# Feed-forward of a decoder layer: gate and up with waits of their own, one maximum over a row of 2048, the integers ahead of the fourth weighing

## The reference

```
def activation_quant(x):
    scale = 127.0 / clip(max(abs(x), axis=-1), EPS, None)
    return clip(round(x * scale), -128.0, 127.0) / scale
gate = bit_linear(x, w_gate)              # 512 -> 2048, x quantised, weights -1, 0, 1 times a scale
up = bit_linear(x, w_up)                  # 512 -> 2048
activated = up * square(relu(gate))
activated = activated * rsqrt(mean(square(activated)) + LN_EPS) * subln_weight
return bit_linear(activated, w_down)      # 2048 -> 512, activated quantised by its greatest magnitude
```

## Time and profile before

| | us |
|---|---|
| median of 3 runs | 669.22 (667.73 to 669.85) |
| the profiled execution, its own time | 666.3 |
| its span | 664.5 |

### The profile page before, as it was taken

One profiled execution on the slowest core, in us unless ns is written; L12 is line 12 of the kernel. 1 busy time (PEld: TensorE's weight loads), 2 busy tenths in 40 slices (PEclk: granted clock), 3 DMA queues, 4 the chain that ended last, 5 costly groups with the idle time before them and its releaser, 6 DMA issues.

```text
span 664.5 us, 10361 instructions
## 1 busy us (share of the span) xinstructions
PE 604.7 (91%) x2741; PEld 336.7 (51%) x2758; DVE 470.2 (71%) x919; ACT 462.7 (70%) x799; POOL 276.8 (42%) x263
## 2 busy tenths in 40 slices
PE   5899999999999998989999999994689999999976
PEld 3535454545364543357777777772244444444332
DVE  3456767575757474536787787789799998989860
ACT  2364666666666665238888889874689888888970
POOL 1000000101010000236777777752587777777761
PEclk9959999999999998889999999996899999999997
DMA  8563144545353627125566566542035354443434
GB/s 300 163 195 87 40 103 151 112 140 125 128 130 122 148 107 161 45 63 166 162 192 170 162 188 185 164 128 79 24 65 120 95 118 98 101 96 87 95 75 100
DMA packets 83752, 82.89 MB, mean 125 GB/s; under 512 B 46160, under 2 KB 57936, under 8 KB 83600
## 3 DMA queue, kind: packets, MB, share of 16 engines
q1 hardware_dynamic: 83728, 82.61, 46.2%
HBM read 47.51 MB, written 4.28 MB: 78 GB/s over the span
## 4 chain that ended last, share of the span: by engine, by line
PE 30%; DVE 8%; POOL 6%; issue 6%; DMA 2%; ACT 1%; DVEq 1%; POOLq 0%; ACTq 0%; SPq 0%
PE ps L713 21%; PE ps L1083 5%; PE ps L1098 4%; POOL big L1340 3%; DMA act8t<-ys 2%; DVE toep L1225 2%; POOL ys L1348 2%; DVE st L1177 1%; DVE qo L766 1%; DVE ot L1263 1%; DVE x_all L1172 1%; POOL r L1336 1%; DVE mb L1229 1%; ACT kv L1122 0%; ACT kv L1120 0%
## 5 line engine op out<-in xcount | busy, mean ns | idle before, releaser
L713 PE MATMUL ps<-kv,toep 128*128 128x288 f32 x640 | 157.3, 409 | 1.2 <-PEq L1411 1.1
L713 PEld LDWEIGHTS ps<-kv,toep 128*128 128x128 f32 x640 | 122.1, 191 | 36.3 <-issue 2.6
L1098 PE MATMUL ps<-wt,xqt 128*128 128x512 bf16 x496 | 119.5, 386 | 14.2 <-DVE toep L1225 6.8
L1340 POOL TENSOR_TENSOR big<-toep,wst 128x512 f32<-128x512 f32 x64 | 83.0, 1299 | 50.3 <-DVE toep L1225 50.3
L401 ACT ACTIVATE big<-ps,kscale 128x512 f32<-128x512 f32 x128 | 84.9, 695 | 13.7 <-PE ps L251 12.0
L251 PE MATMUL ps<-qx,kx 128*128 128x512 f32 x128 | 78.1, 638 | 11.2 <-ACT big L401 10.6
L1098 PEld LDWEIGHTS ps<-wt,xqt 128*128 128x128 bf16 x512 | 49.4, 99 | 75.9 <-DVE toep L1225 13.4
L766 DVE TENSOR_REDUCE qo<-big 128x2048 f32 (+1 forms) x32 | 72.2, 2257 | 0.0
L1083 PE MATMUL ps<-wt,act8t 128*128 128x512 bf16 x255 | 60.7, 392 | 9.0 <-DMA act8t<-ys 8.0
L701 POOL TENSOR_TENSOR kv<-ctx 128x768 f32<-128x768 f32 (+1 forms) x32 | 52.7, 1646 | 37.3 <-PE ps L713 28.4
L755 DVE TENSOR_TENSOR big<-ps,qd 128x1024 f32<-128x1024 f32 x32 | 39.2, 1224 | 37.2 <-ACT ys L845 34.8
(11 more groups left out here) (120 smaller groups left out, 968.2 us busy)
## 6 DMA issues: line engine op xcount, KB each, us to landing
qx<-kv SPq DMA_DIRECT2D x128, 128.0 KB, 2.4
wst<-in_wall SPq DMA_DIRECT2D x12, 1024.0 KB, 6.7
wst<-in_wall SPq DMA_DIRECT2D x48, 256.0 KB, 3.7
toep<-krows SPq DMA_DIRECT2D x32, 256.0 KB, 3.8
ctx<-in_ctxt SPq DMA_DIRECT2D x32, 192.0 KB, 2.6
out_y<-ot SPq DMA_DIRECT2D x16, 256.0 KB, 2.2
conv_part<-qo SPq DMA_DIRECT2D x14, 256.0 KB, 2.8
x_all<-in_x SPq DMA_DIRECT2D x2, 1536.0 KB, 14.6
```

The costliest lines, as they stand in the source:

```text
L713: mm = pe.matmul(m.ps[:, LB * r + lb, :].rearrange("p (b s) -> p b s", s=WIDE)[:, :, 0:PAIRS], m.toep[r][:, d * P:(d + 1) * P], m.kv[r][:, ...
L1098: mm = pe.matmul(bank[:, n % 2, :], xqt[r][:, k, :], wt[:, k, n * C:(n + 1) * C], start=(k == 0), stop=(k == CK - 1))
L1340: nc.gpsimd.tensor_tensor(act_w[r][:, n * C:(n + 1) * C], a[n % 2][:], gb[:, n * C:(n + 1) * C], ALU.mult).then_inc(s_w.sem, 1)
```

## The change

Gate's matmuls wait until relu has read the bank, up's until the product has. The guard of r2 that the old wait gave becomes a wait of its own ahead of the squaring on ACT. The four maxima of 512 columns and the small one over their results become one maximum over the row's 2048 columns, which stands between scale and scale_b. DVE's product of chunk 1 comes ahead of the statistics. POOL's integers of row t-1 come ahead of the fourth weighing of row t.

```
             for n in range(IC):
-                if n >= 2:
-                    wait(pe, s_a, t, n - 1)
-                elif after:
-                    wait(pe, s_a, t - 1, n + 3)
-                for bank, wt, s in ((GB, gate_w, s_g), (UB, up_w, s_u)):
+                for bank, wt, s, free in ((GB, gate_w, s_g, s_rl), (UB, up_w, s_u, s_a)):
+                    if n >= 2:
+                        wait(pe, free, t, n - 1)
+                    elif after:
+                        wait(pe, free, t - 1, n + 3)
                     for k in range(CK):
...
-        def relu(t, n):
+        def relu(t, n, after=True):
             wait(act, s_g, t, n + 1)
             act.activation(rl[n % 2][:], GB[:, n % 2, :], ACT.Relu).then_inc(s_rl.sem, 1)
             wait(act, s_rl, t, n + 1)
+            if n >= 2:
+                wait(act, s_a, t, n - 1)
+            elif after:
+                wait(act, s_a, t - 1, n + 3)
             act.activation(r2[n % 2][:], rl[n % 2][:], ACT.Square).then_inc(s_r2.sem, 1)
...
-        def greatest(t, n, r):
-            wait(dve, s_w, t, n + 1)
-            nc.vector.tensor_reduce(mb4[:, n:n + 1], act_w[r][:, n * C:(n + 1) * C], AX.X, ALU.max,
-                                    apply_absolute_value=True).then_inc(s_mb4.sem, 1)
+        def greatest(t, r):
+            wait(dve, s_w, t, IC)
+            nc.vector.tensor_reduce(mb[:], act_w[r], AX.X, ALU.max, apply_absolute_value=True).then_inc(s_mb.sem, 1)
...
-            wait(dve, s_mb4, t, IC)
-            nc.vector.tensor_reduce(mb[:], mb4[:], AX.X, ALU.max).then_inc(s_mb.sem, 1)
...
             if rows:
                 rows_x2(t + 2)
-            if after:
-                greatest(t - 1, 3, 1 - r)
+            chunk(t, 1, after)
             if rows:
                 rows_stats(t + 2)
-            chunk(t, 1, after)
             if after:
                 scale(t - 1, 1 - r)
             if rows:
                 rows_mean(t + 2)
                 rows_var(t + 2)
             if after:
-                wait(dve, s_mb, t - 1, 1)
-            greatest(t, 0, r)
-            if after:
+                greatest(t - 1, 1 - r)
                 scale_b(t - 1, 1 - r)
             chunk(t, 2)
-            greatest(t, 1, r)
             if rows:
                 rows_norm(t + 2)
             chunk(t, 3)
             if rows:
                 rows_greatest(t + 2)
                 rows_scale(t + 2)
-            greatest(t, 2, r)
...
-        greatest(NT - 1, 3, 1)
+        greatest(NT - 1, 1)
         scale(NT - 1, 1)
...
             weigh(t, 2, r)
-            weigh(t, 3, r)
             if after:
                 integers(t - 1, 1 - r, after=last and final_first)
+            weigh(t, 3, r)
```

More of the change, by code:

```diff
@@ L944, in ffn @@
     act8t = two("act8t", [P, FK, P], BF16)
-    mb4 = sb("mb4", [P, IC])
     cc, sm, var, r4, cr, mb, bm, rb, qs = (sb(n, [P, 1]) for n in (
@@ L960, in ffn @@
     s_x32, s_xq, s_xqt, s_xqe = (sig(n) for n in ("x32", "xq", "xqt", "xqe"))
-    s_g, s_u, s_rl, s_r2, s_a, s_as, s_w, s_mb4 = (sig(n, IC) for n in ("g", "u", "rl", "r2", "a", "as", "w", "mb4"))
+    s_g, s_u, s_rl, s_r2, s_a, s_as, s_w = (sig(n, IC) for n in ("g", "u", "rl", "r2", "a", "as", "w"))
     s_sm, s_cc, s_var, s_r4, s_mb, s_cr, s_bm, s_rb, s_qs, s_fd = (sig(n) for n in (
@@ L1146, in turn @@
         def turn(t, r, after=True, last=True, rows=True, more=True, pair=0, stores=0, final_first=True):
-            relu(t, 0)
+            relu(t, 0, after)
             if after:
                 square(t - 1, 3)
-            relu(t, 1)
+            relu(t, 1, after)
             if more:
```

## The result

| | us |
|---|---|
| before, median of 9 runs | 667.87 (666.72 to 669.85) |
| after, median of 9 runs | 675.72 (671.80 to 678.79) |
| ratio after to before | 1.0112, 95% interval 1.0084 to 1.0139 |
| profiled execution after, and its span | 673.69, 671.9 |

What follows compares the result with a forecast made beforehand. DVE's queue was taken to set the 11.51 us turn. A turn of 10.9 brings turn 14 to -7.4, the tail leaves -5.9, the clock adds 1.4: -4.5, so 669.2 becomes 664.7 us, range 661.3 to 668.3.

Steps and rivals of the forecast that it cites:

- DVE's part: DVE's steady turn: one long maximum of 2.18 covers the 0.53 wait for the root; 10.67 us against 11.54.
- The stop ahead of chunk 3: PE's wait of about 0.6 us a turn for DVE's product of chunk 1, said to go.
- part 4: POOL's integers ahead of weighing 3; the next limit is a ring over DVE and ACT of 10.88 us.
- POOL's ring: Quantise, integers, weighing 3, product 1 and back to quantise: 10.4 us, covered by 0.5; down's wait stays about zero.
- the sign of being wrong: A stop on PE at gate 2 or 3, down or gate 0 in every turn; the period is then theirs.
- the 10.9: The feed-forward's new period in us, 0.6 less than 11.51, with ring 10.88, PE 10.82 and DVE 10.67.
- part 3: PE's split waits: up 3 would start at 6.5, product 1 is done at 5.4, so the 0.6 stop goes.
- Tail: Last turn: bare maximum of 2.2, last root at 641.5, last down product at 651.6: -5.9, giving back 1.5 of 7.4.
- Half of 2.8: Last down product after a gap of 3 us: half clock would cost +2.8, half of it taken, +1.4.
- to the start of turn 4: Head of the feed-forward: earlier rows' integers and down 0 0.8 earlier, together -1.3 us at turn 4's start.
- turns 4 to 13: Ten steady turns at 0.61 us less each, bringing turn 14 to -7.4.
- turn 14 to the end, clock included: The end gives back 1.5 of the 7.4 us, and the clock takes 1.4 more.

Runs made afterwards that it cites:

- e1: The changed kernel with SP's queue issuing the transposing DMA of the integers before the placing of the convolution's rows; 666.97 us, ratio to before 0.9997.
- e2: The changed kernel with POOL's integers back behind the fourth weighing; 669.81 us, ratio to before 1.0035.
- e5: The kernel before with only POOL's integers moved ahead of the fourth weighing; 667.23 us, ratio to before 0.9990.
- e7: The kernel before with only SP's order swapped, transposing DMA first and placing after it; 668.02 us, ratio to before 0.9993.
- e13: The changed kernel with 64 empty instructions on PE ahead of the feed-forward; 675.53 us, ratio to before 1.0110.
- e14: The changed kernel with 128 empty instructions on PE ahead of the feed-forward; 676.69 us, ratio to before 1.0127.
- e6: The changed kernel with SP's order swapped, the last row's maximum by chunk and the last turn's fourth weighing ahead of the integers; 662.50 us, ratio to before 0.9906.
- e9: The changed kernel with 28 and 26 extra matmuls ahead of the last two down products; 675.43 us, ratio to before 1.0101.
- e12: The changed kernel with SP's order swapped and the integers back behind the fourth weighing; 669.59 us, ratio to before 1.0024.
- e4: The changed kernel with PE's old waits ahead of gate and up; 675.26 us, ratio to before 1.0127.
- e11: The kernel before with only DVE's part: one maximum of 2048 in its new place, product 1 ahead of the statistics; 669.84 us, ratio to before 1.0037.
- e3: The kernel before with only the split waits of gate, up and ACT's squaring; 669.11 us, ratio to before 1.0024.
- e10: The changed kernel with SP's order swapped, the tail mended, and 28 and 6 extra matmuls ahead of the last two down products; 660.34 us, ratio to before 0.9907.

## Why the prediction was wrong

- DVE's part held. Long maximum 2.20 against 2.18 taken, no idle for the root, product 1 at 4.5 (near 4.7), quantise 9.6 into the turn (9.8): 567.77 to 577.40.
- The stop ahead of chunk 3 went, as said.
- The step that failed is in part 4 and the paragraph on POOL's ring: "Queued behind them: weighing 3, then weighings 0 and 1 of the next turn, the root, the rows' integers, and on SP's queue the two transposing DMAs", and then "down is due at 7.4. So that wait stays about zero". The integers were said to start at 1.1, take 1.86 and have the DMA behind them at once. They started 0.5 to 0.8 into the turns 6 to 13 and ended near 2.5; but SP's queue had the placing ahead of that DMA, and the placing waits for PE's transposes at 2.3 and takes 0.66. The DMA started at 3.2 and landed at 7.9, and down, due at 7.4, waited in every turn: the sign of being wrong that the prediction itself names. It priced SP's queue by what is behind, not by what is in front. With that link the ring is 3.62 + 1.73 + 0.45 + 0.8 + 4.66 + 0.05 = 11.3. With the median landing of before, 4.4, it is 11.05, an estimate: so the link could have been read in before and put the period over 10.9, and the rest is the slower landing beside the placing. Without the link (e1) the integers start 1.05 to 1.36 into the turn, near the forecast, and the turn is 11.07, 0.17 over the 10.9.
- The wait had no reserve even by the prediction's own numbers: 1.1 + 1.86 and a landing of 4.2 to 6.0 end at 7.2 to 9.0, where it wrote 7.2 to 7.4. Its "30 matmuls less four" in part 3 should be 32 less four, which gives the 6.5 that it used.
- POOL's move helped in the steady turns, as forecast, but only by 0.2 a turn (e2), as it brought the integers in just ahead of the placing's release. In before the same order cost nothing, as DVE's ring was longer (e5, e7). What the move cost lies in the tail, where the fourth weighing stands behind the integers.
- Turn 4's 3.25 were in no case of the prediction: a stop of 2.05 and the half clock behind it (5.31 for 3.63). Runs of the changed kernel with a mean granted clock of 0.951 or 0.952 took 675.51 to 678.79 us, those with 0.954 to 0.956 671.80 to 674.51; the profiles of e13 and e14, with two such stops, have 0.951 and 678.77 and 675.80. That the slower runs had two stops is argued from the clock and the profiles, not shown by a kernel free of the stop alone.
- Tail: start of turn 15 to the last product had +1.8 by the prediction's own times (26.6 against 24.76), measured +2.39. A part of it is that from cr to bm (L1247, L1250) it takes 0.70 (652.08 to 652.78), where before had 0.32 and e6 has 0.32 again; why is not known. e6, which mends the tail, shows the whole price of it in the new order: by the profiles 2.5 to the last product and 2.4 behind it, by its clock.
- Clock: after a gap of 3.50 the last product ran 6.55, mean granted clock 0.54 of full, mostly the 1.2 GHz level; before, 3.61 at the 2.4 GHz level after a gap of 0.94. Half of 2.8 was taken, the whole came. By the Trainium skill (TensorE: Matmul & The Clock Gate, Part 1: The HAM clock gate) a PE that has been idle falls to half rate; here the trace agrees for the gap of 3.50, and e9's extra matmuls in the gap kept the granted clock at 1.00. For shorter gaps the runs show both outcomes: after stops of 2.05 (after) and 2.71 (e12) down took 5.31 and 5.19, after stops of 2.07 (e4), 2.33 (e2) and 2.46 (e11) it took 3.63.

```profile
662.00:668.60 6.60, 6.54 (x16) 2.15 (x16) 0.00 (x0) 0.00 (x0) 0.00 (x0) 0.54 0.01 2
```

The account by stretches of the two profiles:

| stretch | forecast | measured |
|---|---|---|
| ahead of the feed-forward | 0 | +1.83 |
| to the start of turn 4 | -1.3 | -0.92 |
| turns 4 to 13 | -6.1 | +1.63 |
| turn 14 to the end, clock included | +2.9 | +4.86 |
| sum | -4.5 | +7.40 |

The 7.7 of turns 4 to 13 are 3.6 in turn 4 (14.71 against 11.11 in e1), 2.5 by the ring in the nine turns behind it (102.02 against 99.56), and 1.7 by which e1's ten turns of 11.07 stay over the forecast. So the ring through SP's queue, the step that failed, is 2.5 us of the loss, and the larger part, turn 4, is a stop whose cause is open; that the swap takes it away as well is shown, why is not. With SP's order mended (e1) the kernel has -0.6 in the head and -4.4 in the ten turns; the tail and the clock take that back (+2.4 each), and e1 ties with before. Of the 8.7 between e1 and the changed kernel the profiles hold 6.9, of which 6.1 are the ring and turn 4; the rest is between profiled executions and medians.

## What to carry to other kernels

What a step gains by becoming ready earlier ends where its DMA stands, on an in-order queue, behind one that waits for something else: for each moved producer read the queue's order in front of its consumer's issue, with what each entry there waits for. When the bounding ring is cut, add up every other ring through the same engines, the queues among them; here the next was 0.1 shorter (11.3 to 11.4 against 11.46). A merge that is hidden in the steady turns is bare in the last one: keep the split form there.

## What the runs showed that was not expected

- The landing of the transposing DMA is not fixed: 4.27 and 4.28 alone (the changed kernel's at 627.12 and 657.73), 4.66 when the placing (256 KB) was issued just ahead of it, 4.37 to 4.43 when just behind (e1).
- Stops of 2.05 to 2.71 us ahead of down in turn 4, turn 7 or both, in the profiles of eight kernels (the changed one, e2, e4, e9, e11 to e14), and one of 1.45 in turn 6 of e3; none in before, e1, e5, e6, e7 and e10. In the first nine PE waits for this DMA in most turns, by 0.3 to 1.1; in the other six it does so in fewer of the turns 4 to 13 or in none, and by less than 0.3. That the two belong together is not tested, and the cause is open.
- Either hunk alone (waits 1.0024, DVE's order 1.0037) is slower than before; integers alone (0.9990) and SP's swap alone (0.9993) are level. SP's swap with all of the change is level too, and gains 0.9% once the tail is mended: no edit alone shows what they do together.
